# Small SBUF buffers padded or merged so that every buffer begins at a multiple of 128 bytes

## What is computed

```python
x = x + 0.5 * ffn0(layernorm(x))        # silu(x W1 + b1) * (x W2 + b2), then W3, b3; 512 wide, half the weights zero
x = x + attention(layernorm(x))         # 32 heads of 128; q and k RMS-normed over 4096; softmax; Wo, bo
x = x + 0.5 * ffn0(layernorm(x))        # the same weights again
x = x + 0.5 * ffn1(layernorm(x))        # 1376 wide, ternary weights, results truncated to int8 values
x = x + retrieval(layernorm(x))         # 8 of the 32 query heads: (elu(q)+1) M / ((elu(q)+1) z + eps), repeated by 4, then Wo
x = x + 0.5 * ffn1(layernorm(x))
```

## The kernel before, in words

| stream | weights | moving | matmuls |
|---|---|---|---|
| ffn0 up | first or w12 | ln_xT | 2 x 192 (24 of each 192 within the block before) |
| ffn0 down | h | w3 | 2 x 96 |
| projections, Q and K | w (qkv_w) | ln_xT | 1536 |
| projections, V | ln_xT | w (qkv_w) | 768 |
| scores | q, held in ln_xT_lo | k, held in ln_xT_hi | 1536 |
| probs times V (line 1167) | v | pT | 1536 |
| attention output | y | o | 768 |
| ffn1 up | first or f1_w | ln_xT | 2 x 528 |
| ffn1 down | inter | wd | 2 x 176 |
| retrieval queries | first or rt_w | ln_xT | 192 |
| retrieval output | ret | wo | 192 |

## Time and profile before

### The profile page before, as it was taken

The page is one execution under the profiler, slowest core; times in us unless marked ns, Lnnn a source line. Parts: engine busy times, 40 slices in busy tenths (PEclk is TensorE's granted clock), DMA queues, the critical chain, the costliest instruction groups (busy, mean ns, idle before and its releaser), DMA issues. The chain is left out here.

```text
span 2423.0 us, 34736 instructions
## 1 busy us (share of the span) xinstructions
PE 2308.4 (95%) x11044; PEld 1867.0 (77%) x11044; DVE 1737.5 (72%) x2677; ACT 1094.3 (45%) x1782; POOL 1318.2 (54%) x1025
## 2 busy tenths in 40 slices
PE   7899999999889999999999999999999999899998
PEld 5688888888677777777777777777776788687887
DVE  4533333333389999999999999999997565785665
ACT  3222222222165656556556655565564344352442
POOL 4533333223286666666666666666564556673465
PEclk9999999999999999999999999999999999999999
DMA  2244444443311111101111111011110121041120
GB/s 92 83 133 139 146 140 134 144 146 130 117 61 40 61 38 53 61 30 61 52 39 61 47 43 61 30 61 54 37 53 12 46 75 52 12 137 53 57 70 35
DMA packets 91493, 175.34 MB, mean 72 GB/s; under 512 B 8224, under 2 KB 40992, under 8 KB 88096
## 3 DMA queue, kind: packets, MB, share of 16 engines
q1 hardware_dynamic: 91424, 174.46, 21.4%
HBM read 122.00 MB, written 52.43 MB: 72 GB/s over the span
## 5 line engine op out<-in xcount | busy, mean ns | idle before, releaser
L957 POOL TENSOR_TENSOR at_probs<-at_probs,at_rsums 128x1024 f32<-128x1024 f32 x256 | 488.6, 1909 | 429.4 <-DVE at_rsums L1089 429.4
L1012 ACT ACTIVATE at_probs<-ps,at_nbias,rms 128x1024 f32<-128x1024 f32 x256 | 309.2, 1208 | 281.2 <-DVE at_nbias L1076 279.8
L348 PE MATMUL ps<-ln_xT_hi,ln_xT_lo 128*128 128x512 f32 x1488 | 385.0, 394 | 0.0
L1005 ACT ACTIVATE at_pT_hi<-ps 128x512 fp32r<-128x512 f32 x512 | 277.4, 594 | 188.1 <-PE ps L1142 188.1
L769 POOL TENSOR_TENSOR qkv_acc<-qkv_acc,qkv_sq 128x512 f32<-128x512 f32 x128 | 165.4, 1292 | 339.8 <-ACT qkv_sq L680 338.1
L348 PEld LDWEIGHTS ps<-ln_xT_hi,ln_xT_lo 128*128 128x128 f32 x1488 | 279.1, 188 | 64.3
L1084 DVE TENSOR_TENSOR at_pT_lo<-ps,at_pT_hi 128x512 fp32r<-128x512 f32 x512 | 327.0, 680 | 1.7 <-ACT at_pT_hi L1005 1.7
L1074 DVE TENSOR_REDUCE at_maxes<-ps 128x1 f32<-128x1024 f32 x256 | 310.8, 1214 | 20.0 <-PE ps L348 19.9
L1142 PE MATMUL ps<-ident,at_probs 128*128 128x128 f32 x2048 | 273.1, 275 | 25.6 <-DVE at_pT_lo L1084 20.6
L1142 PEld LDWEIGHTS ps<-ident,at_probs 128*128 128x128 f32 x2048 | 235.7, 140 | 76.5 <-DVE at_pT_lo L1084 36.0
L680 ACT ACTIVATE qkv_sq<-qkv_res 128x512 f32<-128x512 f32 x128 | 80.9, 632 | 369.5 <-DVE qkv_res L733 361.4
(11 more groups left out here) (252 smaller groups left out, 4912.3 us busy)
## 6 DMA issues: line engine op xcount, KB each, us to landing
scratch_q<-qkv_res SPq DMA_DIRECT2D x64, 256.0 KB, 2.0
scratch_k<-qkv_res SPq DMA_DIRECT2D x64, 256.0 KB, 2.0
scratch_v<-qkv_res SPq DMA_DIRECT2D x64, 256.0 KB, 2.3
k_raw<-scratch_k SPq DMA_DIRECT2D x32, 512.0 KB, 3.9
q_raw<-scratch_q SPq DMA_DIRECT2D x32, 512.0 KB, 5.0
at_v_raw<-scratch_v SPq DMA_DIRECT2D x32, 512.0 KB, 3.2
qkv_w<-in_Wq SPq DMA_DIRECT2D x8, 1024.0 KB, 4.9
qkv_w<-in_Wk SPq DMA_DIRECT2D x8, 1024.0 KB, 5.0
```

What stands on the lines that cost most here:

```text
L348: last = nc.tensor.matmul(out, s, m, start=(start and n == 0), stop=(stop and n == len(terms) - 1))
L957: nc.gpsimd.tensor_tensor(probs[l % 4][:], probs[l % 4][:], rsums[:, l % 4:l % 4 + 1].broadcast_to([P, TOK]), ALU.mult)\
L1005: nc.scalar.activation(pT2[jp][0][:, 4 * b:4 * b + 4, w * P:(w + 1) * P], T_BANKS[:, b * HALF:(b + 1) * HALF].rearrange("p (k n) -> p k n" ...
L1012: nc.scalar.activation(probs[l % 4][:], scores(l)[:], ACT.Exp, bias=nbias[:, l % 4:l % 4 + 1], scale=rq[:, l % NT:l % NT + 1], accum_out=s ...
```

## The change

Sizes and places of small buffers, nothing else. `whole(n)` rounds a number of 4-byte elements up to a multiple of 32, which is 128 bytes.
- `half`, and the layer norm's var, sd, r0, corr and rstd become slices of one buffer, ln_small (41 elements, so 64). ln_stats gets 8 elements for each token block and uses 6 of them, ln_meanvar is padded to 32.
- rms is padded from 1032 to 1056 elements, b12 of ffn0 from 8 to 32, ms, sd, r0, corr and rs of the projections from 16 to 32 each, maxes, nbias, sums and rsums of attention from 4 to 32 each.
- Retrieval's weight chunks go from 642 to 672 elements (642 are used), and den and rden become slices of the buffer of bq, which gets 32 elements.

No instruction, wait or DMA is added, removed or moved, and none gets another number of elements. The core of the diff:

```diff
+LINE = 32
+
+def whole(n):
+    return (n + LINE - 1) // LINE * LINE
...
-        self.half = ctx.enter_context(nc.sbuf_tensor("half", [P, 1], F32))
         self.ln = LayerNormBuffers(nc, ctx)
+        self.half = self.ln.small[:, 5 * NT:5 * NT + 1]
...
-        self.rms = ctx.enter_context(nc.sbuf_tensor("rms", [P, TOK + NT], F32))
+        self.rms = ctx.enter_context(nc.sbuf_tensor("rms", [P, TOK + whole(NT)], F32))
...
-        self.stats = sb("stats", [P, NT, 6])
-        self.meanvar = sb("meanvar", [P, NT, 2])
-        self.var, self.sd, self.r0, self.corr, self.rstd = (sb(n, [P, NT]) for n in ("var", "sd", "r0", "corr", "rstd"))
+        self.stats = sb("stats", [P, NT, 8])[:, :, 0:6]
+        self.meanvar = sb("meanvar", [P, whole(2 * NT)])[:, 0:2 * NT].rearrange("p (t m) -> p t m", m=2)
+        self.small = sb("small", [P, whole(5 * NT + 1)])
+        self.var, self.sd, self.r0, self.corr, self.rstd = (self.small[:, i * NT:(i + 1) * NT] for i in range(5))
...
-        b12 = sb("b12", [P, 2 * MB0])
+        b12 = sb("b12", [P, whole(2 * MB0)])[:, 0:2 * MB0]
...
-        ms, sd, r0, corr, rs = (sb(n, [P, 2, NT]) for n in ("ms", "sd", "r0", "corr", "rs"))
+        ms, sd, r0, corr, rs = (sb(n, [P, whole(2 * NT)])[:, 0:2 * NT].rearrange("p (a t) -> p a t", a=2)
+                                for n in ("ms", "sd", "r0", "corr", "rs"))
...
-        maxes, nbias, sums, rsums = (sb(n, [P, 4]) for n in ("maxes", "nbias", "sums", "rsums"))
+        maxes, nbias, sums, rsums = (sb(n, [P, whole(4)]) for n in ("maxes", "nbias", "sums", "rsums"))
...
-        w = [core.first] + [Chunk(nc, ctx, f"rt_w{i}", HEADW, raw=raws[i % 2]) for i in range(1, RING)]
-        bq = sb("bq", [P, KVH])
+        w = [core.first] + [Chunk(nc, ctx, f"rt_w{i}", whole(HEADW), raw=raws[i % 2]) for i in range(1, RING)]
+        bq = sb("bq", [P, LINE])
+        den, rden = (bq[:, a:a + 2 * TH].rearrange("p (m t) -> p m t", m=2) for a in (KVH, KVH + 2 * TH))
...
-        den, rden = sb("den", [P, 2, TH]), sb("rden", [P, 2, TH])
```

More of the change, by code:

```diff
@@ L374, in _ @@
                                     base=0, pattern=[[-1, P]], channel_multiplier=1).then_inc(made, 1)
-            nc.gpsimd.memset(core.half[:], 0.5)
+            nc.gpsimd.memset(core.half, 0.5)
             for k in range(ln.STEPS):
@@ L441, in _ @@
         def _(sp):
-            sp.dma_start(b12[:], ins["b12T"]).then_inc(bias_in, 16)
+            sp.dma_start(b12, ins["b12T"]).then_inc(bias_in, 16)
             sp.dma_start(b3[:], ins["b3"].partition_broadcast(P)).then_inc(b3_in, 16)
@@ L455, in _ @@
             pool.wait_ge(b3_in, 16)
-            nc.gpsimd.tensor_tensor(b3[:], b3[:], core.half[:].broadcast_to([P, DM]), ALU.mult).then_inc(biased, 1)
+            nc.gpsimd.tensor_tensor(b3[:], b3[:], core.half.broadcast_to([P, DM]), ALU.mult).then_inc(biased, 1)
             pool.wait_ge(biased, 1)
@@ L683, in _ @@
             act.wait_ge(ms_done, 1)
-            nc.scalar.activation(sd[:], ms[:], ACT.Sqrt).then_inc(sd_done, 1)
+            nc.scalar.activation(sd, ms, ACT.Sqrt).then_inc(sd_done, 1)
             act.wait_ge(kn_done, 1)
@@ L696, in factors @@
                 v.wait_ge(sums_done, 1)
-                nc.vector.tensor_scalar(ms[:], core.bank(6)[:, 0:2 * NT].rearrange("p (a t) -> p a t", a=2),
+                nc.vector.tensor_scalar(ms, core.bank(6)[:, 0:2 * NT].rearrange("p (a t) -> p a t", a=2),
                                         1.0 / INNER, RMS_EPS, ALU.mult, ALU.add).then_inc(ms_done, 1)
                 v.wait_ge(sd_done, 1)
-                nc.vector.reciprocal(r0[:], sd[:]).then_inc(rs_done, 1)
+                nc.vector.reciprocal(r0, sd).then_inc(rs_done, 1)
                 v.wait_ge(rs_done, 1)
-                nc.vector.tensor_tensor(corr[:], ms[:], r0[:], ALU.mult).then_inc(rs_done, 1)
+                nc.vector.tensor_tensor(corr, ms, r0, ALU.mult).then_inc(rs_done, 1)
                 v.wait_ge(rs_done, 2)
-                nc.vector.tensor_tensor(corr[:], corr[:], r0[:], ALU.mult).then_inc(rs_done, 1)
+                nc.vector.tensor_tensor(corr, corr, r0, ALU.mult).then_inc(rs_done, 1)
                 v.wait_ge(rs_done, 3)
-                nc.vector.tensor_scalar(corr[:], corr[:], -0.5, 1.5, ALU.mult, ALU.add).then_inc(rs_done, 1)
+                nc.vector.tensor_scalar(corr, corr, -0.5, 1.5, ALU.mult, ALU.add).then_inc(rs_done, 1)
                 v.wait_ge(rs_done, 4)
-                nc.vector.tensor_tensor(rs[:], r0[:], corr[:], ALU.mult).then_inc(rs_done, 1)
+                nc.vector.tensor_tensor(rs, r0, corr, ALU.mult).then_inc(rs_done, 1)
                 v.wait_ge(rs_done, 5)
@@ L1496, in _ @@
         def _(sp):
-            sp.dma_start(bq[:], ins["bq1T"]).then_inc(bq_in, 16)
+            sp.dma_start(bq[:, 0:KVH], ins["bq1T"]).then_inc(bq_in, 16)
             for h in range(KVH):
```

## The result

The changed kernel takes 2408.0 us, median of 4 runs (2404.3 to 2409.2), against 2423.7 for the kernel before in the same session; the ratio is 0.9931, 95% interval 0.9917 to 0.9945, or 13 to 20 us. The forecast was 2404.1. The profiled execution spans 2407.3 us, 15.7 less than the earlier trace rows.

A forecast was written before the change was run, and what follows sets the result against it. TensorE bounds the projections without a gap and shares the bound with VectorE in attention. Savings of 14.8 + 0.8 + 1.4 + 2.5 = 19.5 us give 2404.1 us; range 2393 to 2427, the likeliest case 2393 to 2413.

The forecast's parts named there:

- The table of remainders: List of matmul streams by both operands' start modulo 128 bytes: same remainder about 226.7 ns, different about 233.
- the second rival: No effect: 233.3 ns has another cause, or the unit is, say, 256 bytes; 2423 us, chance 0.15.
- Projections, 14.8: Q, K and V products: 2240 matmuls each 6.6 ns faster with TensorE never idle, saving 14.8 us.
- ffn0 down, 0.8: Down product of both ffn0 blocks: 192 matmuls by 6.2 ns make 1.2 us, counted as 0.8.
- Retrieval, 1.4: Retrieval: 192 output matmuls save 1.2 us, 180 query matmuls at most 1.1; 1.4 together after waits.
- Attention, 2.5: Attention: score matmuls no longer settle anew, 30 ns per step, two of eight steps counting per head; 2.5 us saved.
- Small buffers, 0: Strided bn_stats output and shared or padded small buffers: no effect, half a microsecond either way.
- full rate: Rival: at remainder 0 streams run one column per cycle, 213.3 ns; 92 us saved, 2332 us, chance 0.12.
- slower: Rival: remainder 0 itself is bad, so streams at 226.7 go to 233.3 ns; 2439 us, chance 0.07.
- The first rival: The full rate rival; with the skill page's 216 ns between starts, its time would be some 15 us above 2332.

The follow-up runs named there:

- the first run: Kernel before with buffer rms 32 elements longer, so weights w begin at 64 modulo 256 as xT does: 2409.7 us, ratio 0.994.
- second: Kernel before with only the shared part's small buffers padded, xT at 0 modulo 128, w still at another remainder: 2426.4 us, ratio 1.0001.
- third runs: Changed kernel with 32 bytes left free ahead of all large buffers, every base at 32 modulo 128, differences kept: 2408.7 us, ratio 0.9929.
- the fourth run: Changed kernel with 128 bytes left free ahead of weights w alone, so w and xT differ by 128 modulo 256: 2424.0 us, ratio 0.9992.

## Why the prediction was right, and where not

**The rule.** "A stream whose two operands begin at the same place modulo 128 bytes settles at 226.7, and one whose operands don't stays at 233.3": the relation was right and the unit wrong. The first, second and third runs show that only the difference counts, the fourth that 128 is a difference like any other. The table of remainders in the prediction could not tell the units apart, because every pair that agreed modulo 128 there agreed modulo 256 too, and every pair that differed, differed in both. The text on the second rival had seen that h and w3 differ modulo 256 but kept it as a rival's condition and priced them at 0.8 all the same. That the change brings w and xT together modulo 256 too is luck as far as the rule goes: for the fourth run's layout the rule promises the same 14.8 us, and the kernel gains nothing. The Trainium skill, page "TensorE: Matmul & The Clock Gate", under its phase DRAIN, describes the reads of the moving operand and of the weights as two independent ports; the measurement decides here: the pace of the stream depends on how the two operands lie to each other.

**Projections, 14.8.** The mechanism was right and the size about right: 884 matmuls in 200 us, as forecast to the unit. The stage gave 12.6 in the profiled execution, with a half-clock spell of 3.0 in it, and 15.4 at equal clock. The term was 0.6 low: the distance before was 233.6 by its own window and not 233.3, which makes 2240 x 6.9 = 15.5. The 16.6 between the kernel before and the first experiment holds 1.2 more, as the opening stretch at half clock was six steps longer in the former.

**ffn0 down, 0.8.** Nothing: h and w3 differ by 128 modulo 256. With the difference mended it is 0.2, as half of the matmuls come in short runs behind a pause and the others' gain goes into the pause behind them.

**Retrieval, 1.4.** The stage did lose 1.4 us, but only 0.8 of it by the alignment, all in the output product; the other 0.6 is the clock. The queries, priced at up to 1.1, gave nothing: the 120 matmuls whose weights are in rt_w take 64.7 us from first to last in both kernels. The prediction counted 180 with weights at other remainders, but heads 0, 3 and 6 of the ring of three take theirs from first, and rt_w1_hi lay where xT does. So 72 of the 192 differed before, and 40 of them, the low parts at 128, still do. All come in runs of a dozen.

**Attention, 2.5.** Nothing: the length stayed within 0.3. The steps went as described up to the last one: scores at 1.36, VectorE's wait down by 2.0 us in 30 heads, 66 ns per head against a forecast 60. The step that failed is "only what TensorE gains between its own last wait and that moment shortens the head": VectorE's gain at that wait has to pass kn before it counts, and kn's end is set by GpSimd, which goes straight from v_lo to probs; a second part is lost behind q_high, and how it is lost there stays open. The prediction had the other engines' large operands at 0 because their rows don't depend on the place, which holds; that a row's length depends on what runs beside it was not weighed, although kn's row of the kernel before, 1268 ns at least and 2484 in the median, said so. With VectorE relieved of one step, or GpSimd of another, the 2 us appear (1.7 and 2.4). "TensorE's wait for VectorE grows" was right: 39.2 to 40.2 in the two rows; the table of steps has it in finer form.

**Small buffers, 0**: no stage shows anything that could be theirs; the first run, without them, comes to 2409.7. **Rivals**: full rate and slower fall on ffn1's unchanged 487 and 443 at remainder 0. The second rival was right in its detail (256, h and w3) and wrong in its total, as w and xT agree modulo 256 after the change. The first rival's "some 15 us" for 216 ns in place of 213.3 is 12 by its own 4596 matmuls outside attention.

Together, at equal clock: 14.8 was worth 15.4, 0.8 nothing, 1.4 was 0.8, 2.5 nothing, which is 16.2 against a measured 15.7 (13 to 20 by the ratio's interval) and a forecast of 19.5. The range held although two terms were empty, since nearly all of the gain came from the one term whose mechanism was right. In the profiled execution the clock took 3.0 us in the projections and probably the 1.3 in ffn1 and gave 0.6 in the retrieval, and the earlier start gave 3.0, so that its 15.7 agrees with this sum by luck in part.

## What to carry to other kernels

Where TensorE has no gap, count its matmuls in a window and compare the distance of starts among streams of one shape: a busy share of 100% hid 3% here. Before padding a whole memory plan, find the one pair of operands that carries the matmuls, and make their difference a multiple of the unit (256 bytes here); one longer buffer gave 15.9 us, and the whole plan, shifted by 32 bytes, 16.9 in the same session. Where two engines wait for each other, look at the range of each step's length: a step that lasts from 1.27 to 2.7 us for the same work can end with its neighbour, as kn does 1.08 us behind probs, and then what is gained ahead of it is lost there until one of the two is relieved. And before crediting a stage with a gain, compare its half-clock time on both sides: it made 0.8 us look like 1.4 here, and 15.4 like 12.6.

## What the hardware showed that was not expected

- TensorE's pace for 512 columns and 128x128 weights follows the difference of the two operands' first addresses modulo 256 bytes: 226.7 ns at 0; 233.3 at 32, 233.0 at 64, 232.5 at 128 and 233.6 at 160. Their own places don't matter (0, 32, 64, and 128 with 128 all gave 226.7). What in the memory does it is open, and so is whether other shapes or types show it.
- Behind a pause of TensorE an aligned stream has its starts 224 to 236 ns apart for one to nine steps before it stands at 226.7, so short runs keep much of the cost whatever their addresses; an aligned stream that follows another without a pause runs at 226.7 at once.
- The half-clock spell behind the 32 one-column matmuls comes in some executions and not in others, at the same work: about 3.0 us lost for 6.8 us at half clock. What decides it stayed open.
- One step of 1.9 us per head, moved from VectorE to ScalarE, gave 39 us in 32 heads, 1.2 us each, more than the alignment of the whole plan.
